# Local attention: softmax weights divided by their sums before the transposition, instead of the output multiplied by spread reciprocals

## The reference, cut to what matters

```python
def local_attention(q, k, v):          # 8 heads of 64, windows of 128 rows
    bq = q.reshape(b, h, w, WINDOW, d) * QK_SCALE
    bk, bv = (look_around(bk), look_around(bv))     # this window and the one before: 256 keys
    sim = jnp.einsum('bhwid,bhwjd->bhwij', bq, bk)
    sim = jnp.where(mask, -jnp.finfo(sim.dtype).max, sim)
    attn = jax.nn.softmax(sim, axis=-1)
    out = jnp.einsum('bhwij,bhwjd->bhwid', attn, bv)
...
q = l2norm(q) * qs; k = l2norm(k) * ksc
q, k = rotary_xpos(q, k)
o = local_attention(q, k, v)
x = x + o @ wo
h = shift_token(x)
...                                     # layer norm
h = h @ w1 + b1
a, g = jnp.split(h, 2, axis=-1)
x = x + (a * jax.nn.gelu(g)) @ w2 + b2
```

## Time and profile before

| | us |
|---|---|
| median of 3 runs | 2881.08 |
| lowest, highest | 2879.59, 2883.12 |
| span of the profiled execution | 2876.6 |
| median less the span | 4.5 |

### The profile page before, as it was taken

One profiled execution on the slowest core, in us unless ns is written; L12 is line 12 of the kernel. 1 busy time (PEld: TensorE's weight loads), 2 busy tenths in 40 slices (PEclk: granted clock), 3 DMA queues, 4 the chain that ended last, 5 costly groups with the idle time before them and its releaser, 6 DMA issues.

```text
span 2876.6 us, 52549 instructions
## 1 busy us (share of the span) xinstructions
PE 2806.9 (98%) x20384; PEld 1887.3 (66%) x20384; DVE 2168.8 (75%) x5059; ACT 1650.4 (57%) x3488; POOL 1055.4 (37%) x1210
## 2 busy tenths in 40 slices
PE   8999999999999999999998899999999999999998
PEld 7777877333333333333335788888888888888887
DVE  7885545788788778877874777777777778888886
ACT  3222332665565656566664676666666766666663
POOL 5343442024113311421322444444445554544442
PEclk9999999999999999999999999999999999999999
DMA  2000010320321222042202100000000100000001
GB/s 80 23 10 23 8 23 3 41 29 11 41 24 18 27 30 28 7 58 24 32 16 76 29 5 5 4 5 5 11 20 26 33 27 5 12 12 12 11 12 61
DMA packets 49149, 66.65 MB, mean 23 GB/s; under 512 B 12590, under 2 KB 37124, under 8 KB 48900
## 3 DMA queue, kind: packets, MB, share of 16 engines
q1 hardware_dynamic: 48900, 63.29, 12.4%
HBM read 24.99 MB, written 8.39 MB: 12 GB/s over the span
## 4 chain that ended last, share of the span: by engine, by line
PE 89%; DVE 5%; ACT 3%; DMA 1%; POOL 1%; issue 1%; SPq 0%; POOLq 0%; ACTq 0%; DVEq 0%
PE ps L1416 17%; PE pw L220 17%; PE ps L220 13%; PE pw L1403 11%; PE ps L1202 6%; PE pw L1202 5%; PE ps L1576 4%; PE pw L1527 3%; PE pw L1489 2%; PE pw L1509 2%; PE ps L1489 1%; PE pw L1352 1%; PE ps L1527 1%; DMA c_qst<-c_mr 1%; PE ps L1386 1%
## 5 line engine op out<-in xcount | busy, mean ns | idle before, releaser
L1707 ACT ACTIVATE c_p<-pw 128x512 f32<-128x512 f32 x1024 | 562.2, 595 | 337.6 <-PE ps L1386 179.7
L1416 PE MATMUL ps<-c_p,c_vals 128*64 128x512 f32 x2048 | 547.7, 618 | 2.9 <-ACT c_p L1707 1.6
L1995 DVE TENSOR_REDUCE c_mx<-ps 128x1 f32<-128x512 f32 x694 | 462.7, 683 | 111.8 <-PE ps L1386 103.6
L1403 PEld LDWEIGHTS pw<-c_qst,c_kst 50*128 50x128 f32 x1024 | 154.8, 185 | 366.3 <-ACT c_p L1707 271.8
L1403 PE MATMUL pw<-c_qst,c_kst 50*128 50x512 f32 x1024 | 384.6, 450 | 7.5 <-DMA c_qst<-c_mr 6.6
L1386 PE MATMUL ps<-c_kst,c_qst 48*128 48x512 f32 x694 | 289.5, 453 | 1.5 <-DVE c_mx L1995 0.8
L1761 ACT ACTIVATE e_sm<-e_sm,e_mx 128x256 f32<-128x256 f32 x512 | 254.0, 500 | 63.5 <-DVE e_mx L2140 63.3
L1995 DVE TENSOR_REDUCE c_mx<-pw 128x1 f32<-128x512 f32 x330 | 225.5, 683 | 45.7 <-PE pw L1386 42.2
L2363 POOL TENSOR_TENSOR e_ss<-e_ss,half 128x16 f32<-128x16 f32 x64 | 186.7, 2917 | 118.4 <-DVE e_ss L2097 104.6
L2260 POOL TENSOR_SCALAR stat<-stat 128x1 f32<-128x1 f32 (+1 forms) x141 | 33.7, 239 | 522.2 <-DVE stat L1867 464.0
L1416 PEld LDWEIGHTS ps<-c_p,c_vals 128*64 128x64 f32 x2048 | 104.3, 135 | 181.6 <-issue 161.3
(11 more groups left out here) (316 smaller groups left out, 6355.6 us busy)
## 6 DMA issues: line engine op xcount, KB each, us to landing
c_kst<-shared SPq DMA_DIRECT2D x192, 64.0 KB
c_qst<-shared SPq DMA_DIRECT2D x64, 128.0 KB
x<-in_L_attn_x SPq DMA_DIRECT2D x8, 512.0 KB, 3.9
c_qst<-shared SPq DMA_DIRECT2D x64, 64.0 KB
keep<-x SPq DMA_DIRECT2D x8, 512.0 KB, 4.0
e_raw<-keep SPq DMA_DIRECT2D x8, 512.0 KB, 3.5
e_hs<-x SPq DMA_DIRECT2D x64, 63.0 KB
out<-x SPq DMA_DIRECT2D x7, 512.0 KB, 5.1
```

Of the source, the lines that this page charges most:

```text
L1403: e.matmul(bank_of("c_s", n, sh, kt, h), c_kst[i][p0:p0 + 50, sh // 2, 128 * kt:128 * kt + 128], c_qst[i][p0:p0 + 50, sh // 2, 512 * h:512 ...
L1416: ins = e.matmul(pv[64 * h:64 * h + 64, :], c_v[:, kt, 33 * hd:33 * hd + 64], p[:, 512 * h:512 * h + 512], start=kt == 0, stop=kt == 7, sk ...
L1707: e.activation(c_p[slot["c_p", (n, sh, kt)]][:, 512 * h:512 * h + 512], bank_of("c_s", n, sh, kt, h), ACT.Exp, scale=0.5).then_inc(SC, 1)
L1995: e.tensor_reduce(c_mx[m % 2][:, qt, h:h + 1], bank_of("c_max", n, sh, qt, h), AX.X, ALU.max).then_inc(VE, 1)
```

## The change

The exponentials are divided by their sums on ACT, in place, before they are transposed. The products that spread the reciprocals, their copy and the multiplication of the output go away; the output is rounded straight from PSUM. The tables of durations and due times have other numbers, so that the order on each engine is another one from the first window of the local attention on. What the first three stages issue, and in which order, is as before.

```diff
-PERIOD, LATE, SPREAD, EPS, LAG, LANDS, FIRST, STEP = 21, 63.09, 1.36, 0.13, 0.05, 2.91, 14.83, 21.95
+PERIOD, LATE, SPREAD, EPS, LAG, LANDS, FIRST, STEP = 21, 62.4047, 1.329, 0.1383, 0.05, 2.91, 14.83, 21.95
-        "act d_exp": 1.2, "dve d_soft": 0.2, "pe d_flip": 0.44, "act d_flip": 0.62, "pe d_rb": 0.95,
-        "act d_rb": 0.62, "pe d_w": 1, "dve d_o": 0.72, "act d_o": 0.66, "dve d_ol": 0.72, "pe d_wo": 1.45,
+        "act d_exp": 1.2, "dve d_soft": 0.2, "act d_norm": 0.9, "pe d_flip": 0.44, "act d_flip": 0.62, 
+        "pe d_w": 1, "act d_o": 0.66, "dve d_ol": 0.72, "pe d_wo": 1.45,
...
-       "pe d_flip0": 3.3, "pe d_flip1": 32.2, "act d_flip0": 33.8, "act d_flip1": -6, "dve d_soft0": 20.2,
+       "pe d_flip0": -1.7, "pe d_flip1": 43, "act d_flip0": 30.2, "act d_flip1": 6.9, "dve d_soft0": 15.5,
...
-                        put("pe", "d_flip", hq, r, after=[("act", "d_exp", *n, hq, r)] + [("pe", "d_flip", *n, hq, 0)] * r,
+                        put("act", "d_norm", hq, r, after=[("dve", "d_soft", *n, hq)] + [("act", "d_norm", *n, hq, 0)] * r)
+                        put("pe", "d_flip", hq, r, after=[("act", "d_norm", *n, hq, r)] + [("pe", "d_flip", *n, hq, 0)] * r,
...
-                    put("dve", "d_soft", hq, after=[("act", "d_exp", *n, hq, 1)] + behind("pe", "d_rb", k=3))
-                    put("pe", "d_w", hq, after=[("act", "d_v", *n), ("act", "d_flip", *n, hq, 1), ("pe", "d_rb", *n)] +
+                    put("dve", "d_soft", hq, after=[("act", "d_exp", *n, hq, 1)])
+                    put("pe", "d_w", hq, after=[("act", "d_v", *n), ("act", "d_flip", *n, hq, 1)] +
...
-                put("pe", "d_rb", after=[("dve", "d_soft", *n, hq) for hq in range(2)], takes=[(bank, "d_rb", *n)])
-                put("act", "d_rb", after=[("pe", "d_rb", *n)] + behind("dve", "d_ol"), gives=[(bank, "d_rb", *n)])
-                put("dve", "d_o", after=[("act", "d_rb", *n), ("pe", "d_w", *n, 1)], gives=[(bank, "d_ob", *n)])
-                put("act", "d_o", after=[("dve", "d_o", *n)] + behind("pe", "d_wo"))
-                put("dve", "d_ol", after=[("act", "d_o", *n)])
+                put("act", "d_o", after=[("pe", "d_w", *n, 1)] + behind("pe", "d_wo"))
+                put("dve", "d_ol", after=[("act", "d_o", *n)], gives=[(bank, "d_ob", *n)])
...
+            def d_norm(l, win, hq, r):
+                sm, mx = [t[slot["d_sm", (l, win, hq)]] for t in (d_sm, d_mx)]
+                w.wait_ge(*dve("d_soft", l, win, hq))
+                for q in range(2 * r, 2 * r + 2):
+                    ins = e.activation(sm[:, q, :], sm[:, q, :], ACT.Copy, scale=mx[:, 2, q:q + 1])
+                ins.then_inc(SC, 1)
...
-                e.activation(d_ot[:, 0, :], d_of[:, :], ACT.Copy).then_inc(SC, 1)
+                e.activation(d_ot[:, 0, :], bank_of("d_ob", l, win), ACT.Copy).then_inc(SC, 1)
...
-                e.reciprocal(d_rp[win % 3][:, 2 * hq:2 * hq + 2, :].rearrange("p h r -> p r h"),
-                             mx[:, 1, :].rearrange("p (r h) -> p r h", r=2)).then_inc(VE, 1)
+                e.reciprocal(mx[:, 2, :], mx[:, 1, :]).then_inc(VE, 1)
...
-                e.tensor_tensor(d_ot[:, 1, :], d_of[:, :], raw32(d_ot[:, 0, :]), ALU.subtract).then_inc(VE, 1)
+                e.tensor_tensor(d_ot[:, 1, :], bank_of("d_ob", l, win), raw32(d_ot[:, 0, :]), ALU.subtract).then_inc(VE, 1)
```

More of the change, by code:

```diff
@@ L41 @@
         "dve n_st a": 0.6, "pool n_st a": 0.8, "dve n_nm a": 0.42}
-BY_HALF = ("d_sim", "d_max", "d_exp", "d_flip", "d_soft", "d_w")
-DUE = {"pe d_qk": 13.8, "act d_qk": -0.3, "dve d_rope": 13.2, "pe d_turn": 3.5, "act d_turn": -15.3, "dve d_ss": 31,
-       "pool d_r": 16.5, "dve d_add": -21.6, "dve d_scale": 2.1, "pe d_v": 15.5, "act d_v": 22.3, "pe d_sim0": 22.8,
[3 rows of a table removed]
-       "act d_o": 43, "dve d_ol": 37.9, "pe d_wo": 21, "dve d_wo": 36.2, "dve n_st": 50, "pool n_st": 38.1,
-       "dve n_nm": 48.7, "d_x": -0.2}
+BY_HALF = ("d_sim", "d_max", "d_exp", "d_flip", "d_soft", "d_norm", "d_w")
+DUE = {"pe d_qk": 11.3, "act d_qk": -13.9, "dve d_rope": 0.4, "pe d_turn": -7.3, "act d_turn": -2, "dve d_ss": 36.3,
+       "pool d_r": 71.1, "dve d_add": -31, "dve d_scale": 3.4, "pe d_v": 12.8, "act d_v": 38.5, "pe d_sim0": 22.7,
[3 rows of a table added]
+       "act d_o": 37.5, "dve d_ol": 38.1, "pe d_wo": -2.8, "dve d_wo": 39.4, "dve n_st": 82.4, "pool n_st": 58,
+       "dve n_nm": 35.9, "d_x": -3.8}
 PACE, NEAR = 16.73, 0.16
@@ L326, in build @@
             d_mx = [sbin(c, f"e_mx{i}", [128, 3, 4]) for i in range(2)]
-            d_rp = [sbin(c, f"e_rp{i}", [128, 4, 2]) for i in range(3)]
             d_pt = [sbin(c, f"e_pt{i}", [128, 2, 2, 2, 128]) for i in range(2)]
@@ L331, in build @@
             d_hn = sbin(c, "e_hn", [128, 4, 256])
-            d_of = sbin(c, "e_of", [128, 512])
             d_hb = shared[:, 6144:8192].rearrange("p (a b n) -> p a b n", a=2, b=2)
@@ L1494, in d_flip @@
                 p, sm = bank_of("d_flip", l, win, hq, r), d_sm[slot["d_sm", (l, win, hq)]]
-                w.wait_ge(*act("d_exp", l, win, hq, r))
+                w.wait_ge(*act("d_norm", l, win, hq, r))
                 for s in freed("d_flip", l, win, hq, r):
@@ L1499, in d_flip @@
                            for h in range(2) for n in range(2)]).then_inc(PE, 1)
-            def d_rb(l, win):
-                p, rp = bank_of("d_rb", l, win), d_rp[win % 3]
-                for hq in range(2):
-                    w.wait_ge(*dve("d_soft", l, win, hq))
-                for s in freed("d_rb", l, win):
-                    w.wait_ge(*s)
-                for h in range(4):
-                    for r in range(2):
-                        ins = e.matmul(p[64 * r:64 * r + 64, 128 * h:128 * h + 128],
-                                       rp[:, h, r:r + 1].broadcast_to([128, 64]), ident[:, :],
-                                       start=True, stop=True, skip_group_check=True)
-                ins.then_inc(PE, 1)
             def d_w(l, win, hq):
@@ L1584, in tensor @@
                       c_ft=c_ft, c_ot=c_ot, c_wo=c_wo, d_x=d_x, d_v=d_v_, d_qk=d_qk, d_turn=d_turn, d_sim=d_sim,
-                      d_flip=d_flip, d_rb=d_rb, d_w=d_w, d_wo=d_wo_, f_x=f_x, f_g=f_g, f_a=f_a, f_down=f_down))
+                      d_flip=d_flip, d_w=d_w, d_wo=d_wo_, f_x=f_x, f_g=f_g, f_a=f_a, f_down=f_down))
         def play(eng, parts):
@@ L1771, in d_flip @@
                              ACT.Copy).then_inc(SC, 1)
-            def d_rb(l, win):
-                n = 32 * l + win
-                if n:
-                    w.wait_ge(*dve("d_ol", *divmod(n - 1, 32)))
-                w.wait_ge(*pe("d_rb", l, win))
-                e.activation(d_of[:, :], bank_of("d_rb", l, win), ACT.Copy).then_inc(SC, 1)
             def d_o(l, win):
@@ L1783, in d_o @@
                     w.wait_ge(*pe("d_wo", *divmod(n - 1, 32)))
-                w.wait_ge(*dve("d_o", l, win))
-                e.activation(d_ot[:, 0, :], d_of[:, :], ACT.Copy).then_inc(SC, 1)
+                w.wait_ge(*pe("d_w", l, win, 1))
+                e.activation(d_ot[:, 0, :], bank_of("d_ob", l, win), ACT.Copy).then_inc(SC, 1)
             def f_x(l, bk, k):
@@ L1811, in scalar @@
                       c_s=c_s, c_o=c_o, c_ot=c_ot, d_x=d_x, d_v=d_v_, d_qk=d_qk, d_turn=d_turn, d_exp=d_exp, d_flip=d_flip,
-                      d_rb=d_rb, d_o=d_o, f_x=f_x, f_hp=f_hp, f_ge=f_ge))
+                      d_norm=d_norm, d_o=d_o, f_x=f_x, f_hp=f_hp, f_ge=f_ge))
         def vector(e):
@@ L2222, in vector @@
                       c_lam=c_lam, c_ft=c_ft, c_n2=c_n2, c_n3=c_n3, c_ot=c_ot, c_wo=c_wo, d_xs=d_xs, d_x=d_x, d_ss=d_ss_,
-                      d_rope=d_rope, d_add=d_add, d_scale=d_scale, d_max=d_max, d_soft=d_soft, d_o=d_o, d_ol=d_ol, d_wo=d_wo_, d_hs=d_hs_, f_x=f_x, f_mul=f_mul,
+                      d_rope=d_rope, d_add=d_add, d_scale=d_scale, d_max=d_max, d_soft=d_soft, d_ol=d_ol, d_wo=d_wo_, d_hs=d_hs_, f_x=f_x, f_mul=f_mul,
                       f_hp=f_hp, f_xl=f_xl, f_hl=f_hl, f_add=f_add))
```

7 lines of the change are left out of this document (removed), and 4 rows, old and new, of the table DUE.

## The result

| | before | after |
|---|---|---|
| median, us | 2881.09 (20 runs) | 2887.05 (20 runs) |
| lowest, highest | 2877.72, 2886.29 | 2880.41, 2891.46 |
| span and granted clock of the profiled execution | 2876.6, 0.993 | 2881.3, 0.987 |

The ratio is 1.0018, 95% interval 1.0011 to 1.0024: the kernel got 0.2% slower (the medians differ by 6.0 us), where 43 us faster was forecast. The median lies outside the range of 2817 to 2864. In the first 1560 us nothing moved (TensorE busy 1525.4 us before, 1524.6 after).

The account below looks back on a forecast made before the run. TensorE was taken to bound the local attention; -59.7 + 3 - 2.5 + 5.6 + 5.6 + 4 + 1.4 = -42.6 us, from 2881.1 to 2838.5, said as 2838; range 2817 to 2864.

Parts of the forecast that it names:

- the forecast's own signs of being wrong: Profile after: divisions above 0.6 us, or TensorE under 95% busy between 1620 and 2750 us, would make the prediction wrong.
- The products that go, -59.7: TensorE, all 64 windows: products spreading the reciprocals go, 0.92 us a window and 1.77 in window 0, -59.7 us.
- The order's own cost on TensorE, +3: TensorE, local attention: 26 more splits between products of different shape at 0.12 us, +3 us, bounds 0 and 8.
- The division: ACT: eight divisions a window, each between 0.31 and 0.51 us, taken as 0.40; ACT has 85% of TensorE's time.
- DVE: DVE: about 1 us less work a window; shorter way to the output projection ends the waits for `e_ot`, -2.5 us.
- The longer way from scores to transposition: Transpositions wait for all four exponentials, reciprocals and two divisions: nine windows short, +5.6 us at start, +5.6 middle, bounds 0 and 25.
- The test that made me trust this count: Same count on the order before: first three windows short by 8.4 us, where the trace has waits of 8.8 us.
- Tight handoffs, +4: ACT's copy of the first half's last transposition, before the value products: 0.06 us a window, 4 us, bounds 0 and 32.
- The end, +1.4: Between last output projection and the last block's first transposition: one feed-forward group less to cover the wait, +1.4 us.
- The slow clock: TensorE: a wait can cost twice, as an idle array falls back to half its clock; no size given.
- Waits at the handoffs. Table loads are not in the planner's model: Rival, chance 0.10: each window loses 0.5 us more on TensorE, 32 us come back, 2870; sign: `e_pt` waits over 20 us.
- The rival of two score tiles: Rival, chance 0.05: loop through both `e_sm` tiles, some 17 us, becomes the bound; slower from 19.8; 2905 at divisions of 0.80.

Follow-up runs that it names:

- the two newly planned orders: Arithmetic of the kernel after, replanned with table loads counted: 2827.14 us; arithmetic of the kernel before, same planner and length of fitting: 2873.34 us.
- one table: Kernel after with Tanh in place of Gelu, so the 97 table loads in the local attention go: 2852.76 us, ratio 0.9893 to the kernel before.
- the order fitted without loads: Arithmetic of the kernel after, new planner counting 0 us for a table load, due times fitted anew: 2924.61 us, ratio 1.015 to the kernel before.

## Why the prediction was wrong, step by step

The profiled span was forecast to go down by 42.6 us, and went up by 4.7. Two steps of the sum failed by most: what the new order costs on TensorE itself, and the waits for ACT, which were counted window by window as if ACT came to each on time. None of the forecast's own signs of being wrong came about (divisions above 0.6 us, TensorE under 95%); TensorE's 96.7% stood between them and the forecast's 97.

- **The products that go, -59.7: right.** 60.9 us of TensorE are gone. Most of it was on the path: 32 of the 42 us that were cut in the kernel before reached the end, and 46 between the two newly planned orders.
- **The order's own cost on TensorE, +3: much too small.** It is 17.8. A split was counted at 0.12 us, read from one group with one change ahead of it; a split makes two, and they cost 0.25 to 0.29. For 26 splits that is 7 us. And I left out that a set of four transpositions standing next to another costs 0.44, one standing alone 0.36: the new order has the sets of the scores in 132 groups, where there were 214, an estimated 7 us more. These two make 14 of the 17.8; what the rest is made of isn't shown. 14 us of the miss are here.
- **The division: right.** 499 ns, between the bounds; a step of 0.40 to the next (four in 1.69 us). The rule of the Trainium skill ("ScalarE: Activation LUTs", section "What ACT_TABLE_LOAD costs"), some 93 ns for an operand with one value per partition, agrees with the trace: 499 against the plain copy's 410. ACT works 81% of the middle stretch, since the kernel takes longer than was forecast.
- **DVE: right.** The remainder takes 686 ns instead of 963, and the waits for `e_ot` (4.1 us in the division of TensorE's time) are gone.
- **"The longer way from scores to transposition", +5.6 at the start and +5.6 in the middle: this step failed.** Its place was right, its size wrong. The waits at these transpositions rose by 29 us, counted as in the table. At the start the listed waits for divided scores rose by 13.4 us (6.3 to 19.7), and the loads have no part in that. In the middle I named windows 6, 10, 30 and 38, and 10, 30 and 38 have the long waits for divided scores (1.35 and 0.51, 1.01, 1.77 and 0.62 us); there the listed rise is 3.2 us (2.5 to 5.7), under the 5.6. What came on top was not in the count: 3.7 us of waits for DVE's rotation in windows 32 and 40, and sets of transpositions that start 0.3 us late in every fourth window, such as 14, 18, 22 and 26, by the start-to-start times; the list doesn't show them. Those windows were counted among the ones that "have 0.5 to 2.4 us to spare, mostly 1.6". With one table nothing is late in windows 14 to 26. I counted each half from its first exponential, as if ACT came to it on time. With a gelu and two loads, 3.3 us, among the exponentials ACT comes late. The loads were in the count as work and not as something that holds up what stands behind it; with one table, 34 us come back.
- **The test that made me trust this count was partly luck.** It gave 8.4 us for the first three windows of the kernel before, against 8.8 in the list. But 2.5 of the 8.8 lie behind 1700 us, at 2173 and about 2319 us, where the count had nothing; the first three windows have 6.3.
- **Tight handoffs, +4: 15.** The same cause: the copy to `e_pt` is short, but stands behind a gelu and a load. The list has 13.2 us of these waits, and 1.3 without loads. (The bound of 32 was called half a copy in each window; 64 times 0.5 us is nearly a whole one.)
- **The end, +1.4: right.** The last block's first transposition waits 2.7 us instead of 0.8.
- **The slow clock: not in the sum.** The rivals said that a wait can cost twice. It did, +9.7 us. The time at 1.2 GHz went from 13.7 us to 41.0, of which 31 at the start.

Together: 14 us in TensorE's own steps, 38 in waits and clock (52.0 measured against 14.1 given), 5 given back, makes the 46 between the forecast and the +3.7 of the table. The rival nearest to what happened was "Waits at the handoffs. Table loads are not in the planner's model", which had a chance of 0.10 and a price of 32 us. Its sign, waits for `e_pt` of over 20 us, did not come: they are 8.6, or 13.2 with those put down to `e_ge`. The price was too low because it stood in place of the other losses and not on top of them.

The rival of two score tiles did not come about: its point was a division of 0.75 us, and the division takes 0.50. The kernel got slower without it. The case for it that I lacked was a loss spread over start, handoffs and changes of shape, none of them large. The order was built from durations in which a load doesn't exist; that it had been harmless before (TensorE at 99%, loads worth some 2 us of 2881, within noise) said nothing of an order in which ACT has 20% more to do.

What stays open: the 5 us of the rest, what holds DVE's rotation up in the new order (the waits for L2090), and why the order fitted without loads is 37 us slower than expected.

## What to carry to other kernels

When an in-order engine stays below its bound, don't count each handoff from a fresh start: carry the helping engine's lateness from one step to the next, with everything in its list, table loads too. A cost that a model leaves out can be free in one order and worth 34 us in the next, so one kernel's good record with that model doesn't carry over. Test a count by the place of each wait and not by its sum. Compare two ways of computing only in orders that were made with the same care for both: here that turned +6 us into -46.

## What the runs showed of the hardware

- A table load takes 1283 ns, and the gelu starts 0.02 us after its end (1764.04 + 1.28, then 1765.34). The Trainium skill ("ScalarE: Activation LUTs", section "What ACT_TABLE_LOAD costs") gives 2.66 us for a switch with its drain; in the trace the steps before and behind a load show no such addition.
- Two changes between 64-column value products and full transpositions: 0.29 us of device time, 0.25 us in TensorE's steps. Four transpositions of scores: 0.36 us to the next start where a 512-column product follows, 0.44 where others of their kind do.
- The 963 ns of the subtraction with both inputs in SBUF are a mean of unlike ones: 64 of 677 to 1737 ns. The 16 that ran with GpSimd idle took 680 to 693; the other 48, beside work of GpSimd, took 1054 in the mean. With one input in PSUM, in the kernel after, all 64 took 671 to 693 ns, though GpSimd worked beside 28 of them for 0.3 us or more. So what the change took away on DVE was the time lost beside GpSimd.
- In the kernel after, the granted clock falls to 1.2 GHz at 1576.5 us, within the wait of 3.63 us, and comes back at 1590.1; there four transpositions take 1.11 us instead of 0.66.
